# A recurrent layer behind a 16-tap convolution: first stage reordered by chunk, two taps moved to VectorE, input products and preparations re-placed

## What is computed

```
K = 16 taps:   x = x + causal_depthwise_conv(x, cond)        # per channel
GRU over time: gi = x_t @ W_ih + b_ih ; gh = h @ W_hh + b_hh
               r = sigmoid(i_r + h_r) ; z = sigmoid(i_z + h_z)
               n = tanh(i_n + r * h_n) ; h = (1 - z) * n + z * h
               x_t = x_t + h
```

## Time and profile before

| | us |
|---|---|
| median of 3 runs | 977.74 (977.53 to 977.78) |
| profiled execution | 977.23 |
| its span | 975.5 |
| outside the span | 1.7 |

### The profile page before, as it was taken

The page is one execution under the profiler, slowest core; times in us unless marked ns, Lnnn a source line. Parts: engine busy times, 40 slices in busy tenths (PEclk is TensorE's granted clock), DMA queues, the critical chain, the costliest instruction groups (busy, mean ns, idle before and its releaser), DMA issues.

```text
span 975.5 us, 65427 instructions
## 1 busy us (share of the span) xinstructions
PE 966.4 (99%) x27165; PEld 806.2 (83%) x27165; DVE 879.4 (90%) x3087; ACT 543.7 (56%) x2309; POOL 614.7 (63%) x1790
## 2 busy tenths in 40 slices
PE   9999999999999999999999999999999999999997
PEld 7799987888888888888888888888888888888775
DVE  8889999999999999999999999999999988887565
ACT  4334555565555655555655655655556555556543
POOL 6656666666666666666666666666666666666642
PEclk9999999999999999999999999999999999999999
DMA  8731001010010101101010010100101010000000
GB/s 307 73 49 36 20 20 37 16 34 21 25 37 16 34 16 33 30 20 34 17 33 26 20 38 16 34 19 26 35 17 33 12 31 20 15 25 5 26 15 13
DMA packets 67608, 32.54 MB, mean 33 GB/s; under 512 B 44528, under 2 KB 65648, under 8 KB 67312
## 3 DMA queue, kind: packets, MB, share of 16 engines
q1 hardware_dynamic: 66880, 28.25, 11.3%
q10 hardware_dynamic: 432, 0.11, 0.0%
HBM read 19.86 MB, written 8.49 MB: 29 GB/s over the span
## 4 chain that ended last, share of the span: by engine, by line
PE 91%; POOL 4%; issue 3%; DVE 2%; ACT 0%; DMA 0%; DVEq 0%; POOLq 0%; ACTq 0%
PE pg L1003 64%; PE pg L768 7%; PE pcv L778 5%; PE pg L778 4%; PE pcv L798 3%; PE pcv L788 3%; PE pg L788 3%; PE pg L758 1%; PE pg L798 1%; POOL nzh L733 1%; DVE hp L1324 1%; POOL sd L472 1%; POOL tz L463 1%; DVE gn L1303 0%; PE pcv L768 0%
## 5 line engine op out<-in xcount | busy, mean ns | idle before, releaser
L1003 PE MATMUL pg<-whh,hp 128*32 128x192 f32 x16384 | 717.4, 326 | 3.5 <-DVE hp L1324 3.0
L1003 PEld LDWEIGHTS pg<-whh,hp 128*32 128x32 f32 x16384 | 530.9, 110 | 125.3 <-DVE hp L1324 14.1
L1254 DVE SCALAR_TENSOR_TENSOR pcv<-xb,cnd,pcv 128x256 f32<-128x256 f32 (+2 forms) x588 | 315.0, 536 | 6.9
L1205 ACT ACTIVATE rz<-gt 128x64 f32<-128x64 f32 x512 | 136.2, 266 | 269.6 <-DVE gt L1299 244.5
L733 POOL TENSOR_TENSOR nzh<-rz,hp 128x32 f32<-128x32 f32 x512 | 157.6, 308 | 173.6 <-ACT rz L1205 172.3
L1299 DVE STREAM_TRANSPOSE gt<-pg 128x128 f32<-128x128 f32 x512 | 161.3, 315 | 44.1 <-PE pg L1003 36.8
L1210 ACT ACTIVATE nzh<-an 128x32 f32<-128x32 f32 x512 | 121.1, 237 | 131.0 <-DVE an L1311 131.0
L1324 DVE TENSOR_TENSOR_SCAN hp<-zcp,nzh 128x96 f32<-128x96 f32 x512 | 173.8, 339 | 11.8 <-ACT nzh L1210 9.4
L1311 DVE TENSOR_TENSOR_SCAN an<-rz,gn 128x64 f32<-128x64 f32 x512 | 153.2, 299 | 26.5 <-ACT rz L1205 25.9
L1207 ACT ACTIVATE zcp<-gt 128x32 f32<-128x32 f32 x512 | 111.0, 217 | 0.0
L1303 DVE STREAM_TRANSPOSE gn<-pg 128x64 f32<-128x64 f32 x512 | 106.8, 209 | 0.0
(11 more groups left out here) (147 smaller groups left out, 1085.2 us busy)
## 6 DMA issues: line engine op xcount, KB each, us to landing
xb<-x SPq DMA_DIRECT2D x96, 94.0 KB, 1.9
out<-x SPq DMA_DIRECT2D x60, 128.0 KB, 1.8
wih<-w_ih SPq DMA_DIRECT2D x4, 768.0 KB, 8.0
whh<-w_hh SPq DMA_DIRECT2D x4, 512.0 KB, 12.1
windows<-x SPq DMA_DIRECT2D x24, 64.0 KB, 3.3
whh<-w_hh SPq DMA_DIRECT2D x4, 256.0 KB, 13.4
xb<-x SPq DMA_DIRECT2D x16, 62.0 KB, 1.9
tz<-taps SPq DMA_DIRECT2D x12, 64.0 KB, 3.5
```

The costliest lines, as they stand in the source:

```text
L1003: i = pe.matmul(gates(t // 2, f)[D * j:D * (j + 1), 0:IN], hp[:, t % 2, 2 * c + 1 - t % 2:2 * c + 3 - t % 2, :, 1].rearrange("p u b -> p ( ...
L1205: act.activation(rz[:, f, :, :, 1].rearrange("p g (c b) -> p (g c) b", b=B), gt[:, f, :, u], ACT.Sigmoid).then_inc(s_rz[f], 1)
L1254: dve.scalar_tensor_tensor(x1_of(c, a, b)[:, lo:hi] if lag == K - 1 else sums, xx[:, c, (K - 1 - lag) * B + lo:(K - 1 - lag) * B + hi], cn ...
```

## The change

`FIRST` runs chunk by chunk, and each of its instructions with lag over 0 waits for the one right before it. TensorE's products of chunk c wait for `8 * (c + 1)` of them instead of all 24. Chunk 3 gets 14 taps on ScalarE and TensorE; the last two (`far`, 32 and 16 columns) are done by VectorE at the end of the first stage, counted by a new semaphore `s_far`. `LATE` is 35. `AHEAD` holds 14 products instead of 11 (8 behind chunk 0 of `w_hh`, 5 behind chunk 1, 1 behind chunk 2), the slots of the steps 2, 3 and 8 one fewer each. The first three instructions of `prepare()` move ahead of step 0 on GpSimd.

```diff
-LATE = 27
+LATE = 35
+NEAR = 14
-        AHEAD = {0: parts(3, 0, 3, 0, 1, 2) + parts(3, 1, 3),
+        AHEAD = {0: parts(3, 0, 3, 0, 1, 2) + parts(3, 1, 3, 0, 1, 2) + parts(2, 0, 3),
...
-        FIRST = [(lag, c) for lag in range(FEW) for c in range(C - 1)]
+        FIRST = [(lag, c) for c in range(C - 1) for lag in range(FEW)]
...
+            pool.wait_ge(s_first, len(FIRST) + len(REST))
+            pool.wait_ge(s_far, K - NEAR)
+            pool.memset(jb[:, :, :], 0.0).then_inc(s_prep, 1)
+            pool.memset(base[:, END:], 0.0).then_inc(s_prep, 1)
+            pool.tensor_copy(base[:, 0:END], bc[:, 0, :]).then_inc(s_prep, 1)
 
             def prepare():
 
-                pool.wait_ge(s_first, len(FIRST) + len(REST))
-                pool.wait_ge(s_c3, 1)
-                pool.memset(jb[:, :, :], 0.0).then_inc(s_prep, 1)
-                pool.memset(base[:, END:], 0.0).then_inc(s_prep, 1)
-                pool.tensor_copy(base[:, 0:END], bc[:, 0, :]).then_inc(s_prep, 1)
...
                 if m < 2 and c < C - 1:
-                    pe.wait_ge(s_first, len(FIRST))
+                    pe.wait_ge(s_first, FEW * (c + 1))
+                if c == C - 1 and 2 * m + 2 > NEAR:
+                    pe.wait_ge(s_far, K - NEAR)
...
-            for lag in range(K):
+            for lag in range(NEAR):
                 pe.wait_ge(s_dg, lag + 1)
...
-            for lag in range(K):
+            for lag in range(NEAR):
                 act.activation(diagonal(lag), eye[:, :], ACT.Copy, scale=cnd[:, C - 1, K - 1 - lag:K - lag]).then_inc(s_dg, 1)
...
                 if lag:
-                    dve.wait_ge(s_first, q - (C - 1) + 1)
+                    dve.wait_ge(s_first, q)
...
+            def far(lag):
+
+                dve.wait_ge(s_ev, 1)
+                if lag > NEAR:
+                    dve.wait_ge(s_far, lag - NEAR)
+                o = x1[:, C - 1, lag * B:TB * B]
+                dve.scalar_tensor_tensor(o, xs[:, C - 1, 0:(TB - lag) * B], cnd[:, C - 1, K - 1 - lag:K - lag],
+                                         o, ALU.mult, ALU.add).then_inc(s_far, 1)
...
             for q in range(len(REST) - LATE, len(REST)):
                 rest(q)
+            for lag in range(NEAR, K):
+                far(lag)
```

More of the change, by code:

```diff
@@ L126, in build @@
         s_xw = {c: sem(f"s_xw{c}") for c in BANDED}
+        s_far = sem("s_far")
         s_xe = sem("s_xe")
@@ L213, in parts @@
             return [(m * H + f) * C + c for c in chunks]
-        AHEAD = {0: parts(3, 0, 3, 0, 1, 2) + parts(3, 1, 3),
[L216 to L221, removed]
+        AHEAD = {0: parts(3, 0, 3, 0, 1, 2) + parts(3, 1, 3, 0, 1, 2) + parts(2, 0, 3),
+                 1: parts(2, 0, 0, 1, 2) + parts(2, 1, 3),
+                 2: parts(2, 1, 0)}
+        IN_SLOT = [parts(2, 1, 1) + parts(4, 0, 3, 0, 1, 2), parts(2, 1, 2) + parts(5, 0, 3, 0, 1), parts(5, 0, 2) + parts(5, 1, 3, 0),
+                   parts(6, 0, 0, 1, 2), parts(6, 0, 3) + parts(4, 1, 3), parts(4, 1, 0, 1), parts(4, 1, 2) + parts(7, 0, 0, 1, 2),
+                   parts(5, 1, 1), parts(5, 1, 2) + parts(6, 1, 0, 1), parts(6, 1, 2), parts(6, 1, 3) + parts(7, 0, 3) + parts(7, 1, 0, 1),
+                   parts(7, 1, 2, 3)]
         def products(t):
@@ L1026, in tap @@
                 return pe.matmul(pcv[0][:, lag * B:TB * B], w, xs[:, C - 1, 0:(TB - lag) * B],
-                                 start=begin, stop=lag == K - 1, skip_group_check=True)
+                                 start=begin, stop=lag == NEAR - 1, skip_group_check=True)
             pe.wait_ge(s_clear, 1)
```

## The result

The changed kernel takes **978.84 us** (median of 22 executions, 978.35 to 979.25); the kernel before, beside it, 977.50 (22 executions, 977.00 to 977.85). The ratio is 1.0014, with an interval of 1.0009 to 1.0020. So the change costs 1.3 us, inside the 0.2% that was set as the bound of no change. The forecast was 979.2, between 978.0 and 980.4, with "no change" as the likeliest. The profiled execution took 978.86, its span is 977.1, against 977.23 and 975.5 before: 1.6 more.

The account below looks back on a forecast made before the run. Step 0 was taken to hang on the DMA of `w_hh`, its delay shifting the chain of 256 steps once. 2.05 + 0.25 - 0.65 - 0.15 = +1.5 on 977.74 gave 979.2 us, range 978.0 to 980.4.

Parts of the forecast that it names:

- step 1: Step 1's `an` scan no longer held up by GpSimd's `weights(0)`: gain 0.65 us (0 to 0.85).
- Part 1: VectorE's `FIRST` taps: neighbour waits add 2.15 us, GpSimd 0.35, so `REST` starts 2.5 later.
- rival A: VectorE's neighbour waits are free, the start stays, steps 1, 4 and 9 gain: -0.8, 976.9 us; chance 0.07.
- Part 2: Rest of VectorE's first stage with `far`: `gt` of step 0 at 25.25 instead of 23.20, cost 2.05 us.
- part 4: GpSimd's two memsets and copy ahead of step 0 delay the first `nzh`: cost 0.25 us (0.1 to 0.45).
- Part 3, the start: TensorE reaches the last `w_hh` chunk at 23.75, 1.15 us later, hidden because VectorE is later by 0.9.
- The condition that I named for this: TensorE's delay shows if the dependent taps cost nearly a microsecond less and the transposes stay at 16.7.
- Part 3, the slots: Fewer products in TensorE's step slots recover only its lateness: gain 0.15 us (0 to 0.2).
- this sign: Prediction is wrong if the steps from 2 on differ from before by more than the 0.2 us counted.

Follow-up runs that it names:

- experiment 3: Changed kernel with GpSimd's small copies moved ahead of its three large memsets: 978.49 us, ratio to the kernel before 1.0009.
- experiment 2: Changed kernel with `FIRST` in tap order, each tap still waiting for its neighbour, TensorE waiting for all 24: 981.46 us, ratio to the kernel before 1.0034.
- experiment 5: Changed kernel with all 16 taps of chunk 3 on ScalarE and TensorE again, no `far`: 978.21 us, ratio to the kernel before 1.0008.
- experiment 6: Kernel before with only the new product tables, 14 ahead and fewer in the slots: 977.78 us, ratio to the kernel before 1.0004.
- 7: Changed kernel with `FIRST` in tap order, its old waits, `LATE` 30 and GpSimd's copies ahead of its memsets: 976.39 us, ratio to the kernel before 0.9990.
- experiment 4: Kernel before with only two memsets and the copy of `prepare()` moved ahead of step 0 on GpSimd: 976.97 us, ratio 0.9994.
- 1: Changed kernel with `FIRST` back in tap order, waits three places back, `LATE` 30: 976.40 us, ratio to the kernel before 0.9990.
- 8: Changed kernel with old tap order, `LATE` 30, GpSimd's copies first, 12 products ahead, slots of steps 2 and 3 full: 976.92 us, ratio 0.9994.

## Why the prediction was right, point by point

The parts against their forecasts, read from the profiled executions (the first row is what makes up most of the second and is not added to the sum):

| | forecast | measured |
|---|---|---|
| 24 taps of `FIRST`, longer by | 2.50 | 2.66 |
| `gt` of step 0 later | 2.05 | 2.40 |
| GpSimd ahead of `nzh` | 0.25 | 0.20 |
| step 1 | -0.65 | -0.64 |
| slots | -0.15 | -0.41, of which 0.20 is a pause in before's execution |
| sum | +1.5 | +1.55 (step 13 starts 1.54 later) |

**Part 1** held in its mechanism and was a little short in size. A chunk without GpSimd takes 8.26 - 5.75 = 2.51, where I had 2.45, which makes 0.18 in three chunks. The gaps are the 0.035 of the forecast; the taps themselves last about 0.01 longer than in before. That is not the wait: in the changed kernel the 112-wide taps last 0.334 in mean in `FIRST`, where they wait for the neighbour, and in `REST`, where they don't; before they lasted 0.325 and 0.322. Why is open. The stretch by GpSimd came out at 0.3 where I took 0.35 (experiment 3). The starts are 0.39 to 0.37 apart at the wide end; rival A, in which the waits are free, is refuted, and experiment 2 shows that the wait alone does it. The Trainium skill, page "VectorE: DVE Perf Modes", section "The DRAIN you can't avoid", has a semaphore after each operation at no extra cost; here a wait on the neighbour costs 0.12 per tap at 128 columns (0.38 from start to start instead of 0.263).

**Part 2.** Of the 0.35 by which `gt` came later than forecast, 0.17 is no part of the change: the input `xs` landed later in this execution, 5.75 instead of 5.58. It was between 5.57 and 6.10 in the ten profiled executions. The other 0.18 is part 1's. The cost of `far` was 0.42 in my working and 0.51 in experiment 5: its second tap, which waits on two semaphores, starts 0.36 behind the first (0.25 long, then a gap of 0.10), where I had 0.285. Two slips in the working change nothing: the lower bound of part 2 is 2.05 - 0.25 = 1.8, not 1.7, and 25.33 + 0.96 of part 4 is 26.29, not 26.33.

**Part 3, the start.** The products ahead stand 9, 4 and 1 behind the three chunks (72, 32 and 8 loads), not 8, 5 and 1 as the words on the change said; the sum, which goes by their number, isn't touched. TensorE reached the last chunk at 23.85 (forecast 23.75) and was hidden behind VectorE, as said. The condition that I named for this, cheaper taps, is what experiments 6 and 7 show: then `gt` waits for TensorE, 1.94 and 0.34.

**Part 3, the slots,** measured 0.41, where I had 0.15 and called 0.2 the most. The prediction had said that it is wrong if the steps from 2 on differ from before by more than that 0.2, so by this sign it failed. The rows show what stands behind it, and half of the 0.41 is not the change. Nearly all the excess is step 8: 3.99 before, 3.68 after. First before, weight loads and then matmuls (timelines of short windows, 52.38 to 52.5, 52.42 to 56 and 52.5 to 52.56, so that the 64 loads come apart):

```profile
52.30 0.11 PEld L1003 LDWEIGHTS pg<-whh,hp 128*32 128x32 f32 x1
...
52.55 2.43 PEld L1003 LDWEIGHTS pg<-whh,hp 128*32 128x32 f32 x63
...
52.30 0.24 PE L1018 MATMUL pcv<-tz,windows 128*32 128x64 f32 x4
52.55 0.36 PE L1003 MATMUL pg<-whh,hp 128*32 128x192 f32 x2
```

and after:

```profile
54.14 2.46 PEld L1007 LDWEIGHTS pg<-whh,hp 128*32 128x32 f32 x64
...
54.19 2.78 PE L1007 MATMUL pg<-whh,hp 128*32 128x192 f32 x64
```

Before, one weight load of the step runs, the last four matmuls of the work in front have started by 52.32, and then nothing starts until 52.55, though nothing in the profile holds TensorE up. The other 63 loads take 2.43, as in any step. After, the first matmul starts 0.05 behind its load, so the pause costs 0.20. It is the pause at a fixed count of the last section: experiment 4, which has the old slots too, has it at the same load with 0.55, and its step 8 takes 4.34. Without the pauses the old step 8 takes 3.79 in both, and with one product fewer it takes 3.67 or 3.68 in the seven other experiments. So the product gives 0.11, where I had at most 0.12, and the excess was one pause in one execution.

What is left of the slots is 0.21, at the edge of my range. Step 9 is the other part of it: 3.93 before and 3.92 in experiment 4, 3.81 to 3.83 in all kernels with one product fewer in the slot of step 8. There the lateness does sit in the matmuls:

```profile
56.28 2.60 PEld L1003 LDWEIGHTS pg<-whh,hp 128*32 128x32 f32 x64
...
56.45 2.81 PE L1003 MATMUL pg<-whh,hp 128*32 128x192 f32 x64
```

Before, the first matmul of step 9 starts 0.17 behind its load, since matmuls of the products still stand in front; after, both start at 57.82. I had read TensorE's lateness from the weight loads alone, and this second part of it was not in my working. That is the step of the working that failed here, by 0.11. The steps 10 to 12 lose as much again (+1.43 at step 10, +1.54 at step 13), and no run says why.

**Part 4 and step 1** came out as forecast, and experiment 4 shows the 0.60 with nothing else changed. What I hadn't seen is that this gain and the slots hang together: split alone, steps 2 and 3 take 3.90 and give 0.13 back; with three products in their slots they take 3.75 and 3.85.

**The total** was 0.36 above the measured median. 0.24 of this is the base: the three executions that I had to go by had a median of 977.74, the 22 later ones 977.50. The shift itself was forecast at +1.5 and is +1.34 by the medians and +1.55 at step 13 of the profiled pair. In that pair part 1 was 0.18 too small and `xs` landed 0.17 later, against 0.20 for the pause in before's execution. That these cancel so nearly is luck; what is not luck is the sign, the waits as the cause, and step 1.

## What to carry to other kernels

A wait on the instruction directly ahead costs VectorE time even where no data calls for it; interleave independent chains so that the wait names one further back (three back was free here, two was not tried), and before ordering work chunk by chunk to release a consumer early, price the waits that this adds: here they cost 2.7 us, and the earlier release bought at most 1.4 of it back, by the estimate under experiment 2 only 0.3. A transfer of work to an engine is priced where that engine is the one waited for: two small taps cost 0.5 us at the end of VectorE's stage and relieved an engine with time to spare. How late TensorE is must be read from its matmuls too, not from its weight loads alone, and before a difference in one step is put down to a change, the traces of other kernels with the same step must show it too: 0.20 of the 0.31 here was one pause in one execution.

## What the runs showed of the hardware

- **A neighbour's wait.** Taps whose wait names the place three back start 0.263 apart at 128 columns; with a wait on the place before they start at their duration plus 0.035, also when the data is three places old (experiment 2). With waits on two semaphores, as the second `far` tap has them, the gap was 0.10.
- **GpSimd and VectorE.** The page "SBUF — State Buffer" of the Trainium skill, section "Who interferes with whom", has the shared port as a lock for a whole instruction. The runs add that back-to-back two-input taps keep GpSimd out for many instructions: 6.24 for four copies before, 5.83 for a single 96-wide subtraction in experiment 6, against 0.82 for the copies and 0.39 for the subtraction beside the dependent chain. The price for VectorE of letting it in was 0.3 in all (experiment 3).
- **Pauses of TensorE at a fixed count.** Some executions show weight loads that nothing holds up pausing for 0.1 to 0.7. They do so at the same counts of loads from the first `xs` diagonal on, in kernels with different code there: behind the 207th in experiments 1 and 6 (0.47 and 0.35), behind the 1099th in before and experiment 4 (0.14 and 0.49 of idling between the loads, 0.20 and 0.55 until the matmuls go on), and behind the 1353rd in 1, 4, 5, 6 and 8 (at 61.3 to 62.3 us, 0.17 to 0.68; 0.11 in before, the changed kernel and 3). The DMA records of the same traces name a likely cause. Queue q8, of the kind `instruction`, moves 16 KB at a time, and each of these pauses ended 1.3 to 1.5 us after the latest such transfer did (in experiment 6 it ended at 60.84 and the loads went on at 62.31). In none of the ten traces did one of these three loads start less than 1.28 us after it. That fits a supply of instructions that comes late at times. The Trainium skill, page "Runtime: NRT & Kernel Launch", section "Instruction fetch mechanics", says that engines fetch their instructions in blocks of 256, mostly hidden. The times agree with a fetch that is not always hidden; no run here varied it, so the cause is not shown. Such pauses and the landing of `xs` and `w_hh` differ between the profiled executions, and a single profiled execution must be read with them in mind.
